# Attention and BitLinear block on eight cores: weight loads ahead of the phase barrier, and another order of the first loads

## The chip, the cores and the metric

One Trainium2 chip, eight cores. Each core computes one of the eight sequences of the batch by itself, with the same program. The metric is the device time of the slowest core, in microseconds (us), as the median of several executions.

## The reference

For each sequence x (4096 tokens, width 1024, f32) the block computes causal attention without separate projections, and a feed-forward part with quantized weights and activations, each followed by a layer norm without gain:

```
encR   = x @ R
A      = softmax(encR @ x.T + causal mask)
x1     = layernorm(x + A @ x)
h      = gelu(bitlinear(x1, W1, b1))          # 1024 -> 4096
out    = layernorm(x1 + bitlinear(h, W2, b2)) # 4096 -> 1024

bitlinear(x, W, b):
    w_scale = max(mean(|W|), 1e-5)
    Wq = clip(round(W / w_scale), -1, 1) * w_scale
    x_scale = max(max over the row |x|, 1e-5)
    xq = clip(round(x * 127 / x_scale), -128, 127) * x_scale / 127
    return xq @ Wq.T + b
```

## The kernel before

The program is written out for five engines (PE, DVE, ACT, POOL, SP) by a small builder. `b.op` puts an instruction on an engine, `b.dma` puts a transfer on the queue of SP ("sync"), ACT ("scalar") or POOL ("gpsimd"). Each names the regions it reads and writes, and the builder makes waits from them: a reader waits for the last writers, a writer for writers and readers, an `accum_writes` only for readers. Each engine runs its list in order, so what is written first also waits first. DMAs take their semaphores in turn from a pool of 7 (SP, POOL) or 5 (ACT), and a DMA waits until the one that used its semaphore before has landed. `b.barrier()` makes every engine wait for all instructions and for all DMAs put down so far; its list of DMA counts is taken at its place in the program (`_pool_targets`).

The sequence is cut into 32 tiles of 128 tokens and 8 groups of 512 (group g holds tokens 512g to 512g+511).

**Start.** For group g, `emit_enc_loads(g)` loads four tiles token-major to bf16 (`etm(k)`, POOL's queue, which converts from f32), `emit_enc_stores(g)` writes them to `enc_bf` in HBM, and `emit_enc_transp(g)` reads them back feature-major with eight DMA transposes (`efm(c)` of group g); stores and transposes are on SP's queue. R is brought to a bf16 layout in HBM, `r_bfT`, in eight steps: POOL loads a row block (to `rstage` or `rstage2`, in turn), ACT's queue stores it. `Rcol(0)` and `Rcol(1)` are two buffers for blocks of `r_bfT`, loaded on SP; the first load waits for all eight stores.

**Attention (lines 629 to 665).** Tiles run in the order 4, 5, ..., 31, 0, 1, 2, 3 (`order`, with SKIP = 4), and the groups in the order 1, 2, ..., 7, 0 (`mstream`). At each fourth tile, `emit_encR` computes x @ R for a group in eight e-steps: Rcol times `efm` (L531), eight matmuls each. The first one is for group 1, so it needs Rcol(0) and the eight transposes of group 1. Scores (L546) need `efm` of all groups up to the tile's own; the exponentials go to `A_sb`, are transposed on PE (L575) and multiplied with `etm` (L592, L598). The residual tile comes into `eres`, `emit_epiA` (L606 to L626) writes y1 = x + A x to `y1pre_h`, on SP, from `y1p`.

**Preparation of the weights.** `drain_prep` puts 130 steps between the tiles: W1 and W2 are read once for the mean of their absolute values (loads to `wslot`, DVE L414), then again to be rounded (L452, L456, L459) and stored as bf16 to `w1q_h` and `w2q_h`, with loads and stores on POOL's queue. The steps of W2's rounding come last, and the last of them stand behind the last tile.

**Turn.** Lines 667 to 680: the barrier; then on POOL the bias rows; on SP the eight loads of W1 (`w1tb(d)`, 1 MB each, over the place of the `etm` tiles 4d to 4d+3); and on SP and ACT in turn the eight loads of W2 (1 MB each, the k-th over the place of `efm(k)`). Then ACT takes logarithm and exponential of the variances (L681, L683), and the feed-forward part begins with the loads of `y1t(0)` and `y1t(1)` (lines 869 to 873). `y1t(0)` has the place of `eres(0)`, `y1t(1)` that of `eres(1)`.

**Feed-forward part.** For each tile: `emit_quant` on DVE (L697 to L736), PE transposes, `emit_mm1_half` (8 matmuls L757 with W1 and one with the bias row, L763, to each group of 512 outputs; then Gelu on ACT, L768, and a maximum on DVE, L772), `emit_roundh`, transposes, `emit_mm2` with W2 (L823, L827), `emit_epiB`. Mm1 of tile i+1 is put ahead of mm2 of tile i. The last stage normalizes and writes the output.

The barrier's list of targets, which both versions share:

```
def _pool_targets(self):
    t = []
    for q, pool in self.pools.items():
        for j, s in enumerate(pool["sems"]):
            uses = (pool["n"] - 1 - j) // len(pool["sems"]) + 1 \
                if pool["n"] > j else 0
            if uses > 0:
                t.append((s, 16 * uses))
    return t
```

Of the kernel before, what the change touches and what calls it, by code (L numbers as in the profile page):

```python
# [160 lines left out]
def build_nc(NT=32, npart=None):  # L161
# [28 lines left out]
    with stack:  # L190
# [16 lines left out]
        b = Builder(nc, stack)  # L207
# [26 lines left out]
        def Rcol(s):  # L234
            return bf_med[:, abase + 2048 + 1024 * s:abase + 2048 + 1024 * (s + 1)]
# [122 lines left out]
        b.dma("gpsimd", mask_sb[:, :], maskc[:, :], writes=["mask"])  # L358
        emit_enc_loads(SKIP // 4 if NT >= 8 else 0)
        b.dma("sync", ident[:, :], identi[:, :], writes=["ident"])  # L360
        b.dma("sync", ones_sb[:, :], ones_i[:, :], writes=["ones"])
        for d in range(8):
# [6 lines left out]
                  reads=[rg], accum_writes=["rbfT"])  # L369
        g1st = SKIP // 4 if NT >= 8 else 0  # L370
        emit_enc_loads(1 - g1st)
        emit_enc_loads(2)
        emit_enc_loads(3)
        emit_enc_stores(g1st)
        emit_enc_transp(g1st)
        b.dma("sync", Rcol(0), r_bfT[0], reads=["rbfT"], writes=["Rcol0"])
        emit_enc_stores(1 - g1st)
        emit_enc_transp(1 - g1st)
        emit_enc_stores(2)
# [87 lines left out]
        k = 0  # L467
# [198 lines left out]

        b.barrier()
        b.dma("gpsimd", b1row2, b1bc[0:2, :], writes=["b1row2"])
        b.dma("gpsimd", b2row2, b2bc[0:2, :], writes=["b2row2"])
        for d in range(8):  # L670
            b.dma("sync", w1tb(d), w1q_h[128 * d:128 * (d + 1), :],
                  reads=["w1qh"], writes=[f"w1q{d}"])
        for k in range(8):
            dst = bf_big[:, 32768 + 4096 * k:32768 + 4096 * (k + 1)].rearrange(
                "p (r c) -> p r c", r=4)
            src = w2q_h[512 * k:512 * (k + 1), :].rearrange(
                "(r p) c -> p r c", r=4, p=128)
            b.dma("sync" if k % 2 == 0 else "scalar", dst, src,
                  reads=["w2qh"],
                  writes=[f"w2q{4 * k + j}" for j in range(4)])  # L680
        b.op("scalar", lambda s: s.activation(lnu[:, 0:NT], uA[:, 0:NT], AF.Ln),  # L681
# [158 lines left out]
        def emit_epiB(i):  # L840
# [27 lines left out]

        b.dma("gpsimd", y1t(0), y1pre_h[0:128, :], reads=["y1h0"],
              writes=["y1t0"])  # L870
        if NT > 1:
            b.dma("gpsimd", y1t(1), y1pre_h[128:256, :], reads=["y1h1"],
                  writes=["y1t1"])
        emit_quant(0)
# [100 lines left out]
```

How the kernel before makes its waits and increments, by code:

```python
            def go(eng):  # L144
                for waits, fn, incspec in self.ops[name]:
                    for sem, val in waits:
                        eng.wait_ge(sem, val)
                    if fn is None:
                        continue
                    inst = fn(eng)
                    if incspec is not None:
                        inst.then_inc(incspec[0], incspec[1])
```

## Time and profile before

| | us |
|---|---|
| time, median of 3 runs | 2499.88 |
| lowest and highest of the 3 | 2493.76, 2558.49 |
| execution that was profiled: time | 2494.65 |
| the same: span of the slowest core (core 0) | 2493.1 |
| the same: spans of the other cores | 2474.4 to 2490.7 |

The profile is of core 0 in one execution; its times count from the core's first instruction. The span and the execution's own time differ by 1.55 us, which lie around the instructions. A span is read in three parts here: the start to about 131 us, the attention part to about 1065, the turn to about 1130, and the feed-forward part and the output behind it.

In the rows, L110 is the builder's line for all plain DMAs and L108 for transposes, so a DMA is known by what it moves: "enc_bf<-bf_big" is a store of a tile, "bf_med<-r_bfT" a load of Rcol, "bf_big<-w1q_h" a load of W1. SPq, ACTq and POOL rows of DMAs are the time to issue them, not to move them. q0 is the queue of POOL, q1 that of SP, q10 that of ACT.

### The profile page before, as it was taken

The numbers are of one execution on the slowest core, as the hardware profiler recorded it, in microseconds if no ns is written. First come the engines' busy times: TensorE is split into PE (matmuls) and PEld (weight loads), VectorE is DVE, ScalarE is ACT, GpSimd is POOL, SyncE is SP. The second block draws the span as 40 slices with busy tenths as digits, with TensorE's granted clock in tenths as the row PEclk, the third lists the DMA queues.
The fourth block names the chain that finished last, engine by engine and source line by source line (L and its number), as shares of the span: only waits on it lengthen the run. The fifth ranks groups of instructions, "written<-read, shape, count | busy, mean of one in ns | idle before, by whom it ended". The sixth has DMA issues, their size and how long they took to land.

```text
span 2493.1 us, 27352 instructions; the slowest of 8 cores (2474.4 to 2493.1 us)
## 1 busy us (share of the span) xinstructions
PE 1847.4 (74%) x8840; PEld 798.3 (32%) x9016; DVE 974.2 (39%) x1941; ACT 641.9 (26%) x1271; POOL 169.2 (7%) x303
## 2 busy tenths in 40 slices
PE   0257778887896985117998989998899998988930
PEld 0123233343342432003333333333333343333310
DVE  0042241324232332425445454554545455454422
ACT  0022232232231321003323232232323323232210
POOL 2011111101111111110000000000000000000000
PEclk9878899998998998558999999999999999999975
DMA  9676746546656453573000000000000000000038
GB/s 153 157 199 199 202 168 170 178 106 142 119 134 159 102 144 97 139 242 125 26 13 26 26 14 26 13 26 26 14 26 13 26 14 26 26 14 26 5 125 288
DMA packets 124027, 232.77 MB, mean 93 GB/s; under 512 B 52076, under 2 KB 52204, under 8 KB 122862
## 3 DMA queue, kind: packets, MB, share of 16 engines
q0 software_dynamic: 42832, 128.20, 20.4%
q1 hardware_dynamic: 66016, 88.14, 11.2%
q10 hardware_dynamic: 15040, 14.68, 2.1%
q8 instruction: 75, 1.23, 0.2%
q14 instruction: 64, 0.52, 0.1%
HBM read 164.11 MB, written 69.21 MB: 94 GB/s over the span
## 4 chain that ended last, share of the span: by engine, by line
PE 60%; DMA 21%; issue 7%; DVE 6%; ACT 4%; SPq 1%; POOL 1%; DVEq 0%; ACTq 0%; another core or an unknown queue 0%; POOLq 0%
PE psc L757 16%; PE pav L827 9%; PE pav L823 9%; PE psc L546 6%; DMA bf_med<-r_bfT 6%; PE ptp L575 5%; PE psc L531 4%; PE pav L592 4%; PE pav L598 3%; PE psc L763 3%; DMA w1q_h<-f_big 3%; DMA w2q_h<-f_big 3%; DMA bf_med<-y2pre_h 3%; ACT bf_med L582 2%; DMA f_big<-w1t 2%
## 5 line engine op out<-in xcount | busy, mean ns | idle before, releaser
L757 PE MATMUL psc<-bf_big,bf_med 128*128 128x512 bf16 x1984 | 484.6, 383 | 10.0 <-DMA bf_big<-w1q_h 5.9
L827 PE MATMUL pav<-bf_big,bf_med 128*128 128x512 bf16 x1023 | 397.0, 388 | 4.6 <-ACT bf_med L582 1.3
L823 PE MATMUL pav<-bf_big,bf_med 128*128 128x512 bf16 x977 | 379.3, 388 | 1.0 <-ACT bf_med L582 0.9
L531 PE MATMUL psc<-bf_big,bf_med 128*128 128x512 bf16 x502 | 156.1, 470 | 212.0 <-DMA bf_med<-r_bfT 207.3
L546 PE MATMUL psc<-bf_big,bf_med 128*128 128x512 bf16 x1126 | 280.4, 390 | 1.5 <-issue 0.2
L575 PE MATMUL ptp<-ident,bf_med 128*128 128x128 bf16 x1808 | 169.9, 222 | 129.5 <-ACT bf_med L582 64.5
L768 ACT ACTIVATE f_big<-psc,stats 128x512 f32<-128x512 f32 x256 | 176.0, 687 | 345.8 <-PE psc L763 338.3
L772 DVE TENSOR_REDUCE stats<-f_big 128x1 f32<-128x512 f32 x256 | 169.5, 683 | 231.7 <-ACT f_big L768 231.7
L757 PEld LDWEIGHTS psc<-bf_big,bf_med 128*128 128x128 bf16 x2048 | 181.5, 98 | 239.0 <-issue 57.0
L559 ACT ACTIVATE bf_med<-psc,stats 128x512 bf16<-128x512 f32 x144 | 99.2, 689 | 384.5 <-DVE psc L554 189.5
L575 PEld LDWEIGHTS ptp<-ident,bf_med 128*128 128x128 bf16 x1808 | 118.1, 98 | 206.4 <-issue 174.9
L554 DVE TENSOR_TENSOR psc<-psc,mask_sb 128x512 f32<-128x512 f32 x32 | 22.3, 696 | 412.9 <-PE psc L546 318.8
L582 ACT COPY bf_med<-ptp 128x512 bf16<-128x512 bf16 x320 | 172.4, 587 | 22.9 <-PE ptp L575 9.7
L592 PE MATMUL pav<-bf_big,bf_med 128*128 128x512 bf16 x221 | 87.3, 395 | 113.1 <-ACT bf_med L585 99.8
L851 ACT ACTIVATE f_big<-bf_med 128x1024 f32<-128x1024 bf16 x32 | 33.8, 1056 | 519.4 <-DVE bf_med L846 519.4
L846 DVE SCALAR_TENSOR_TENSOR bf_med<-pav,stats,f_big 128x1024 bf16<-128x1024 f32 x32 | 41.1, 1284 | 321.5 <-PE ptp L807 271.5
L546 PEld LDWEIGHTS psc<-bf_big,bf_med 128*128 128x128 bf16 x1152 | 114.1, 100 | 135.1 <-issue 14.9
L531 PEld LDWEIGHTS psc<-bf_big,bf_med 128*128 128x128 bf16 x512 | 55.9, 115 | 309.1 <-issue 281.2
L823 PEld LDWEIGHTS pav<-bf_big,bf_med 128*128 128x128 bf16 x1024 | 102.5, 100 | 125.8 <-issue 13.9
L827 PEld LDWEIGHTS pav<-bf_big,bf_med 128*128 128x128 bf16 x1024 | 102.4, 100 | 122.9 <-issue 10.2
L592 PE MATMUL pav<-bf_big,b1b 128*128 128x512 bf16 x293 | 112.1, 382 | 20.7 <-ACT b1b L585 18.4
L763 PE MATMUL psc<-b1b,rows 2*128 2x512 bf16 x256 | 98.6, 385 | 32.3 <-ACT rows L744 32.2
(112 smaller groups left out, 1538.1 us busy)
## 6 DMA issues: line engine op xcount, KB each, us to landing
f_big<-w1t POOLq DMA_DIRECT2D x64, 512.0 KB, 5.7
f_big<-w2t POOLq DMA_DIRECT2D x64, 512.0 KB, 5.0
f_big<-enc POOLq DMA_DIRECT2D x32, 512.0 KB, 6.4
bf_med<-r_bfT SPq DMA_DIRECT2D x64, 256.0 KB, 4.5
y1pre_h<-f_big SPq DMA_DIRECT2D x32, 512.0 KB, 2.9
f_big<-y1pre_h POOLq DMA_DIRECT2D x32, 512.0 KB, 3.8
out<-f_big SPq DMA_DIRECT2D x32, 512.0 KB, 3.9
bf_big<-enc POOLq DMA_DIRECT2D x32, 256.0 KB, 11.5
```

Of the source, the lines that this page charges most:

```text
L531: lambda t, e=e, d=d, cur=cur, qlo=qlo, bk=bk: t.matmul(psc[bk][:, :], Rcol(cur)[:, 128 * d:128 * (d + 1)], efm(d, qlo, qlo + 512), start= ...
L546: lambda t, e=e, sup=sup, bank=bank, qi=qi: t.matmul(psc[bank][:, :], encR(e)[:, 128 * (qi % 4):128 * (qi % 4 + 1)], efm(e, 512 * sup, 512 ...
L559: s.activation(A_sb(p)[:, 512 * sup:512 * (sup + 1)], psc[bank][:, :], AF.Exp, bias=bcn, accum_out=sums4[:, sup:sup + 1]),
L575: b.op("tensor", lambda t, j=j, bb=bb: t.transpose(ptp[pk][:, 128 * j:128 * (j + 1)], src_ap[:, 128 * bb:128 * (bb + 1)], ident[:, :]), re ...
L582: b.op("scalar", lambda s, n=n: s.copy(dst2, ptp[pk][:, 0:n]), reads=[f"ptp{pk}"], accum_writes=[dst_region])
L592: b.op("tensor", lambda t, j=j, bb=bb, g=g, nb=nb: t.matmul(pav[:, 0:512], ATg(g)[:, 128 * j:128 * (j + 1)], etm(bb)[:, 0:512], start=(bb ...
L757: b.op("tensor", lambda t, d=d, s4=s4, sup=sup: t.matmul(psc[s4][:, :], xq_fm[:, 128 * d:128 * (d + 1)], w1tb(d)[:, 512 * sup:512 * (sup + ...
L763: b.op("tensor", lambda t, s4=s4, sup=sup, i=i: t.matmul(psc[s4][:, :], s1row2(i % 2), b1row2[:, 512 * sup:512 * (sup + 1)], start=False, ...
L768: b.op("scalar", lambda s, s4=s4, sup=sup, i=i: s.activation(hbuf(512 * sup, 512 * (sup + 1)), psc[s4][:, :], AF.Gelu, scale=s1c[:, i % 2: ...
L772: b.op("vector", lambda v, sup=sup: v.reduce_max(habs[:, sup:sup + 1], hbuf(512 * sup, 512 * (sup + 1)), axis=AXX, apply_absolute_value=True),
L823: b.op("tensor", lambda t, c=c: t.matmul(pav[:, 0:512], hq_fm[:, 128 * c:128 * (c + 1)], w2tb(c)[:, 0:512], start=(c == 0), stop=False), r ...
L827: b.op("tensor", lambda t, c=c: t.matmul(pav[:, 512:1024], hq_fm[:, 128 * c:128 * (c + 1)], w2tb(c)[:, 512:1024], start=(c == 0), stop=False),
```

## The change

It has two parts. At the turn, the loads of the bias rows, of W1 and of W2 are put down ahead of the barrier, and so are the loads of `y1t(0)` and `y1t(1)`, which stood at the beginning of the feed-forward part. As no barrier stands between them and the attention part, they name the regions whose place they take: the `ATG` and `rstage2` buffers, `eres`, the `etm` tiles and the `efm` blocks. At the start, group 0 is loaded first and once more behind R, then group 1; and group 0 is stored and transposed ahead of the first Rcol load, group 1 behind it. The order of the tiles and of `emit_encR` is the same.

```
--- before.py
+++ after.py
@@ -356,7 +356,7 @@
                       transpose=True)
 
         b.dma("gpsimd", mask_sb[:, :], maskc[:, :], writes=["mask"])
-        emit_enc_loads(SKIP // 4 if NT >= 8 else 0)
+        emit_enc_loads(0)
         b.dma("sync", ident[:, :], identi[:, :], writes=["ident"])
         b.dma("sync", ones_sb[:, :], ones_i[:, :], writes=["ones"])
         for d in range(8):
@@ -367,15 +367,15 @@
                   r_bfT[:, :, 128 * d:128 * (d + 1)].transpose([1, 0, 2]),
                   stg.rearrange("p (e j) -> p e j", e=8),
                   reads=[rg], accum_writes=["rbfT"])
-        g1st = SKIP // 4 if NT >= 8 else 0
-        emit_enc_loads(1 - g1st)
+        emit_enc_loads(0)
+        emit_enc_loads(1)
+        emit_enc_stores(0)
+        emit_enc_transp(0)
+        b.dma("sync", Rcol(0), r_bfT[0], reads=["rbfT"], writes=["Rcol0"])
         emit_enc_loads(2)
+        emit_enc_stores(1)
+        emit_enc_transp(1)
         emit_enc_loads(3)
-        emit_enc_stores(g1st)
-        emit_enc_transp(g1st)
-        b.dma("sync", Rcol(0), r_bfT[0], reads=["rbfT"], writes=["Rcol0"])
-        emit_enc_stores(1 - g1st)
-        emit_enc_transp(1 - g1st)
         emit_enc_stores(2)
         b.dma("gpsimd", eres(0), enc[128 * order[0]:128 * (order[0] + 1), :],
               writes=["eres0"])
@@ -664,12 +664,19 @@
             drain_prep((oi + 1) / (1.0 * NT))
         drain_prep(1.0)
 
-        b.barrier()
-        b.dma("gpsimd", b1row2, b1bc[0:2, :], writes=["b1row2"])
+        b.dma("gpsimd", b1row2, b1bc[0:2, :],
+              writes=["b1row2"] + [f"ATG{s}" for s in range(2, 8)]
+              + ["rstage2"])
         b.dma("gpsimd", b2row2, b2bc[0:2, :], writes=["b2row2"])
+        b.dma("gpsimd", y1t(0), y1pre_h[0:128, :], reads=["y1h0"],
+              writes=["y1t0", "eres0"])
+        if NT > 1:
+            b.dma("gpsimd", y1t(1), y1pre_h[128:256, :], reads=["y1h1"],
+                  writes=["y1t1", "eres1"])
         for d in range(8):
             b.dma("sync", w1tb(d), w1q_h[128 * d:128 * (d + 1), :],
-                  reads=["w1qh"], writes=[f"w1q{d}"])
+                  reads=["w1qh"],
+                  writes=[f"w1q{d}"] + [f"etm{k}" for k in range(4 * d, 4 * d + 4)])
         for k in range(8):
             dst = bf_big[:, 32768 + 4096 * k:32768 + 4096 * (k + 1)].rearrange(
                 "p (r c) -> p r c", r=4)
@@ -677,7 +684,9 @@
                 "(r p) c -> p r c", r=4, p=128)
             b.dma("sync" if k % 2 == 0 else "scalar", dst, src,
                   reads=["w2qh"],
-                  writes=[f"w2q{4 * k + j}" for j in range(4)])
+                  writes=[f"w2q{4 * k + j}" for j in range(4)]
+                  + [f"efm{k}g{g}" for g in range(NG)])
+        b.barrier()
         b.op("scalar", lambda s: s.activation(lnu[:, 0:NT], uA[:, 0:NT], AF.Ln),
              reads=["uA"], writes=["lnu"])
         b.op("scalar", lambda s: s.activation(rstdA[:, 0:NT], lnu[:, 0:NT],
@@ -866,11 +875,6 @@
             b.dma("sync", y2pre_h[128 * i:128 * (i + 1), :], y2st(i % 2),
                   reads=[f"y2st{i % 2}"], writes=[f"y2h{i}"])
 
-        b.dma("gpsimd", y1t(0), y1pre_h[0:128, :], reads=["y1h0"],
-              writes=["y1t0"])
-        if NT > 1:
-            b.dma("gpsimd", y1t(1), y1pre_h[128:256, :], reads=["y1h1"],
-                  writes=["y1t1"])
         emit_quant(0)
         emit_xqT(0)
         emit_s1rows(0)
```

The instructions as they now stand, at the places that matter. First POOL's queue at the start, a piece of the difference; "bf_med<-r_mat" and "b1b<-r_mat" are the last two loads of R, "bf_big<-enc" are loads of encoding tiles, "f_big<-enc" is the first residual tile:

```order
 L110 DMA bf_med<-r_mat 128x1024
 L110 DMA b1b<-r_mat 128x1024
-L110 DMA bf_big<-enc 128x1024 x12
+L110 DMA bf_big<-enc 128x1024 x16
 L110 DMA f_big<-enc 128x1024
 L110 DMA bf_big<-enc 128x1024 x4
```

Four more tiles are loaded behind R, sixteen where there were twelve.

Next SP's queue at the start, a piece of the difference with the semaphores that are waited for. The names in it don't tell the group: the four stores are of group 1 before and of group 0 now.

```order
 L110 DMA ident<-identi 128x128
 L110 DMA ones_sb<-ones_i 128x1
-L110 DMA enc_bf<-bf_big 128x1024 [waits dp_gpsimd1]
-L110 DMA enc_bf<-bf_big 128x1024 [waits dp_gpsimd2]
-L110 DMA enc_bf<-bf_big 128x1024 [waits dp_gpsimd3]
-L110 DMA enc_bf<-bf_big 128x1024 [waits dp_gpsimd4]
+L110 DMA enc_bf<-bf_big 128x1024 [waits dp_gpsimd6]
+L110 DMA enc_bf<-bf_big 128x1024 [waits dp_gpsimd0]
+L110 DMA enc_bf<-bf_big 128x1024 [waits dp_gpsimd1]
+L110 DMA enc_bf<-bf_big 128x1024 [waits dp_gpsimd2]
 L108 DMA_TRANSPOSE bf_big<-enc_bf 128x512 [waits dp_sync2,dp_sync3,dp_sync4,dp_sync5]
 L108 DMA_TRANSPOSE bf_big<-enc_bf 128x512 [waits dp_sync0]
```

The kinds and their order on SP are the same in both; the first stores waited for POOL's transfers 1 to 4 (the mask is 0), the first loads of all, and now wait for its transfers 13 to 16, which are the second loads of group 0 behind R.

Last ACT's list at the turn, before:

```order
L110 DMA bf_big<-w2q_h 128x4x1024 x3
L681 ACTIVATE stats<-stats 128x32
L683 ACTIVATE stats<-stats 128x32 [waits es_scalar]
L582 COPY bf_med<-ptp 128x512 [waits es_tensor] x2
L744 COPY rows<-ptp 2x128 [waits es_tensor]
```

and now:

```order
L110 DMA bf_big<-w2q_h 128x4x1024 [waits dp_scalar4,dp_sync1,dp_sync2,dp_sync0]
L110 DMA bf_big<-w2q_h 128x4x1024 [waits dp_scalar0,dp_sync4,dp_sync3,dp_sync2]
L110 DMA bf_big<-w2q_h 128x4x1024 [waits dp_sync4]
L690 ACTIVATE stats<-stats 128x32 [waits es_scalar,es_vector,es_tensor,dp_sync0,dp_sync1,dp_sync2,dp_sync3,dp_sync4,dp_sync5,dp_sync6,dp_gpsimd3,dp_gpsimd4,dp_gpsimd5,dp_gpsimd6,dp_scalar0,dp_scalar1,dp_scalar2,dp_scalar3,dp_scalar4]
L692 ACTIVATE stats<-stats 128x32 [waits es_scalar]
L582 COPY bf_med<-ptp 128x512 [waits es_tensor] x2
```

The long list of waits is the barrier's. Before, it stood at ACT's first load of W2; now it stands at the logarithm behind the loads, and it holds all semaphores of SP's and ACT's queues, on which the weights arrive. The first DVE instruction behind the barrier has such a list too.

## Rows read from the trace of the kernel before

**Rows 1.** The page: its head, and section 4, the chain's shares by engine.
```profile
span 2493.1 us, 27352 instructions; the slowest of 8 cores (2474.4 to 2493.1 us)
...
PE 60%; DMA 21%; issue 7%; DVE 6%; ACT 4%; SPq 1%; POOL 1%; DVEq 0%; ACTq 0%; another core or an unknown queue 0%; POOLq 0%
```

**Rows 2.** Chain of waits, 40 to 135 us: start, length, what.
```profile
48.90 29.65 DMA r_bfT<-b1b
...
106.85 5.77 PE psc L531 x16
...
131.30 1.23 DVE stats L414
```

**Rows 3.** Timeline, 0 to 135 us: start, length, engine, line, operation, [idle before <-releaser].
```profile
19.36 11.35 SPq L108 DMA_TRANSPOSE bf_big<-enc_bf  x8
...
42.88 3.18 POOL L110 DMA_DIRECT2D bf_big<-enc  x6
...
78.72 0.34 SPq L110 DMA_DIRECT2D bf_med<-r_bfT  x1
...
86.65 3.57 PE L531 MATMUL psc<-bf_big,bf_med 128*128 128x512 bf16 x8 [86.65 <-DMA bf_med<-r_bfT]
88.83 10.25 SPq L108 DMA_TRANSPOSE bf_big<-enc_bf  x8
...
101.71 21.11 SPq L110 DMA_DIRECT2D bf_med<-r_bfT  x8
```

**Rows 4.** DMA queues, 50 to 60 us: packets, MB, share of 16 engines.
```profile
q0 software_dynamic: 820, 1.49, 96.4%
q10 hardware_dynamic: 799, 0.20, 14.7%
```

**Rows 5.** The same, 20 to 30 us.
```profile
q0 software_dynamic: 288, 0.52, 41.1%
q1 hardware_dynamic: 2720, 0.66, 38.4%
```

**Rows 6.** The same, 90 to 100 us.
```profile
q1 hardware_dynamic: 4222, 1.02, 54.3%
```

**Rows 7.** Windows: length, busy (x) of PE, PEld, DVE, ACT, POOL, then PEclk, DMA share, GB/s.
```profile
1088.00:1092.00 4.00, 0.00 (x0) 0.00 (x0) 0.00 (x0) 0.00 (x0) 2.64 (x5) 0.50 0.68 184
...
1130.00:1140.00 10.00, 10.00 (x40) 3.63 (x39) 4.24 (x6) 4.00 (x6) 0.00 (x0) 0.91 1.05 387
1140.00:1144.00 4.00, 3.95 (x18) 1.42 (x17) 2.74 (x14) 1.21 (x2) 0.00 (x0) 1.00 0.53 193
```

**Rows 8.** Chain of waits, 1080 to 1130 us; its columns as in rows 2.
```profile
1083.89 3.62 DMA y1pre_h<-f_big
```

**Rows 9.** Timeline, 1064 to 1158 us; its columns as in rows 3.
```profile
1064.77 0.58 PE L598 MATMUL pav<-bf_big,bf_med 128*128 128x512 bf16 x1
...
1088.03 6.11 SPq L110 DMA_DIRECT2D bf_big<-w1q_h  x8
1088.30 20.44 ACTq L110 DMA_DIRECT2D bf_big<-w2q_h  x4
...
1108.79 0.23 ACT L681 ACTIVATE stats<-stats 128x32 f32<-128x32 f32 x1 [23.67 <-issue]
...
1119.06 2.68 PE L757 MATMUL psc<-bf_big,bf_med 128*128 128x512 bf16 x6 [0.33 <-ACT bf_med L582]
...
1128.54 0.60 PE L763 MATMUL psc<-b1b,rows 2*128 2x512 bf16 x1
...
1132.24 0.38 PE L763 MATMUL psc<-b1b,rows 2*128 2x512 bf16 x1
...
1150.72 3.59 PE L757 MATMUL psc<-bf_big,bf_med 128*128 128x512 bf16 x8
...
1154.25 0.60 PE L763 MATMUL psc<-b1b,rows 2*128 2x512 bf16 x1
...
1157.05 0.38 PE L763 MATMUL psc<-b1b,rows 2*128 2x512 bf16 x1
```

## The prediction

> **What bounds the kernel now.** I read the page first, then the chain of waits, then the timeline at the two places that the change touches, and last the DMA queues there. The page gives PE 60% of the chain that ended last and DMA 21% [rows 1]. These DMA stretches sit at the start and at the turn from attention to the feed-forward part.
>
> At the start the chain runs through the last store of the transposed R, 29.65 us on its way, then through SP's own issues, and PE's second e-step begins at 106.85 [rows 2]. The timeline shows why. The transposes of group 1 were issued at 19.36, long before anyone needed them. Rcol(0) goes out at 78.72 when the R store has landed, PE runs one e-step at 86.65, and then it waits: Rcol(1) is queued on SP behind the stores and eight transposes of group 0 and leaves at 101.71 [rows 3]. Everything later hangs on this. DVE's first weight scan starts at 131.30, behind the first scores [rows 2], and the preparation chain follows it through the whole attention part.
>
> At the turn, PE's last attention matmul begins at 1064.77, but DVE, the weight stores and the last y1 store go on; SP's y1 store is issued at 1083.89 and lands 3.62 later, at 1087.5 [rows 8], and the barrier opens at 1088.03. Then 16 MB of weights come in. ACT is held by issuing its four loads until 1108.79, quantization follows, PE starts at 1119.06 and is paced by w1 until its first group closes at 1128.54 [rows 9]. The weights keep the queues full into the window from 1140 to 1144 [rows 7]; I take 1144 for the last landing: half of them land behind running matmuls. That is the cover which the change takes away.
>
> **The change at the turn.** The weight loads now stand ahead of the barrier, and the barrier collects the latest count of every DMA semaphore. So the first instruction behind it waits for all 16 MB, where before it waited for none of them. Step by step, in the times of this execution:
> - Start of the loads. On SP they are still behind the last y1 store, so they leave at 1083.89 + 0.4 = 1084.3 and not at 1065, where their tiles come free; before, 1088.03. The second half, w2, still waits for the last w2 store. That buys at most 3.7 us. At least it buys what the first 4 us of loading moved before, 184 GB/s x 4 us = 0.74 MB, at the late rate of 387 GB/s: 1.9 us [rows 7]. I take 3: last landing at 1141.
> - Barrier. Before, the y1 store landed at 1087.5 and ACT went on at 1088.30, 0.8 later. Now ACT goes on at 1141.8 with Ln and Exp.
> - Quantization. From 1108.79 to PE's first w1 matmul at 1119.06 was 10.3 us [rows 9]; nothing of it can be done ahead now, since DVE and ACT both stand at the barrier. PE starts at 1152.1.
> - First group. PE has idled since 1065, its granted clock was 0.50 in such a stretch [rows 7] (1.2 GHz of the two levels), and the next group after an idle PE closed 3.5 us after it began (1150.72 to 1154.25 [rows 9]). It closes at 1155.6; before at 1128.54: +27.1.
> - The next group took 3.70 us before (1128.54 to 1132.24) and takes 2.80 after such a start (1154.25 to 1157.05) [rows 9]: -0.9.
>
> Sum: +26, from 24 (3.7 us saved and a little more) to 30. The earlier loads of y1t(0), y1t(1) and the bias rows are worth nothing: they land well before 1141. Taking ACT's 20.44 us of issuing out of the way of Ln is worth nothing either, as ACT now waits for the landings themselves. The POOL, SP and ACT queues hold nothing else that anybody waits for.
>
> **The change at the start.** The order of tiles is unchanged, so PE still needs group 1 first. But now group 0 is loaded first, loaded again behind R, and stored and transposed ahead of Rcol(0) and of group 1. SP's first store waits for the second load, so SP does nothing between 9 and about 47.
> - Gain. The R chain runs without stores and transposes beside it. I take 4 us (bounds 0 and 6): the flood of encoding loads, before from 42.88 [rows 3], begins near 39.
> - Four more loads. One tile is 128 packets, and POOL's queue moved 820 packets in 10 us: 1.56 us a tile, 6.2 us in all [rows 4]. POOL's backlog was 20 loads before (12 tiles, the residual, 4 tiles, 3 weight blocks: 2560 packets, 31 us at this rate, after a slow beginning at 42.88 and with the last ones of twice the size), and I put its end at 84; now 84 - 4 + 6 + 2 (the stores of group 0 beside it) = 88.
> - Transposes of group 0, from about 59, beside that backlog. While it was full, the ACT queue's small packets moved one for one with POOL's, 799 to 820 [rows 4]. One for one, at some 73 per us with three queues, 29 us move about 2100 of the 4096 packets. The other 2000 go at the free rate of 422 per us [rows 6], 5 us: done at 93.
> - Rcol(0) and the stores of group 1 stand behind them in the same queue: about 5 us, 98. From there to Rcol(1) it is as before, 88.83 to 101.71 = 12.9 [rows 3]: 111, so +9.
> - The e = 0 matmuls, before done under this wait, now wait for group 1's transposes and end just before Rcol(1) arrives. They stay hidden; reloading their buffer waits for them, at most 1 us.
>
> Low end: the transposes slip through, Rcol(0) leaves when R has landed, and the R chain is 4 us earlier: -4. High end: they hardly move until 88, end at 98, and with the 18 us behind them give 116, +15, with 2 for the buffer: +17. I take +9, since the row with a full POOL queue is the nearest.
>
> The Trainium skill, *DMA: Bandwidth & Descriptors*, "Queues, rings and completion order", says that a DMA engine goes round its queues by whole packets of about 9 to 17 descriptors, not one by one. The row of R's store shows one small packet for one of POOL's, so the trace does not bear it out there; for transposes I can't exclude it, and by it the start would cost about nothing (first rival).
>
> **Sum.** 26 + 9 = +35. On the execution profiled, 2494.65 us, that is 2530; on the median shown, 2499.88, it is 2535. I take 2533. A measurement of this kernel tells about 2% (50 us) from no change, so this is a loss that stays inside.
>
> **Rivals.**
> 1. *Transposes pass the backlog.* For it: between 20 and 30 us they moved 2720 packets against POOL's 288 [rows 5]. Against it: POOL had only two loads under way then and was idle in part. The start costs 0, the turn 26: 2494.65 + 26 = 2521. Chance 0.24.
> 2. *Slower by over 2%: one queue, one backlog.* SP's queue is in order, so anything that holds group 0's transposes holds R, group 1 and the first scores. If POOL's backlog lasts to 95 (R's store, stores and transposes all taking turns) and the transposes run only after it, 95 + 10 + 18 = 123, +21, and with the turn at its high end of 30: +51. From +50 it decides: 2494.65 + 51 = 2546 on this execution, 2551 on the median. Chance 0.12.
> 3. *Faster: the barrier's new wait is empty.* If it did not cover the loads, or they were issued at 1065 in the shadow of the last weight steps, PE would start on w1's own landing, 3.7 us earlier than before, and with the quicker R chain at the start 4 more: 2494.65 - 8 = 2487. Against it: the barrier takes the counts at its own place in the program, and SP stands at the y1 store until 1083.89 [rows 8]. Chance 0.05.
>
> **Chances.** Forecast (+28 to +45) 0.59, rivals 0.24, 0.12, 0.05. The range for 8 in 10 takes in most of rival 1 and stops where rival 2 begins to be rare: 2514 to 2553. By over 2% slower: 0.12; by over 2% faster: 0.01 (only rival 3 together with something unseen); the rest within 2%.
>
> **What would show it.** Right: no PE instruction from the last attention matmul until some 10 us after the last weight has landed; ACT's Ln at or after 1141 plus the shift of the start; SP's first store past 45; Rcol(1) issued near 111; twenty-four loads in POOL's backlog. Between 131 and 1065 all rows should keep their distances, shifted by the same 9 us; from the first group of the feed-forward part on too. Wrong: DVE's quantization before the weights have landed (rival 3), or Rcol(1) at 98 to 103 (rival 1), or past 120 (rival 2). A shift that shrinks or grows in the middle of the attention part would say that the preparation chain is not tied to the start as I read it.

## The result, and the profile after

The changed kernel takes 2531.37 us (median of 10 runs, 2522.61 to 2592.24); before, run beside it, 2515.86 (10 runs, 2491.59 to 2622.16). The ratio is 1.0145, with a 95% interval of 1.0124 to 1.0166: on the 2499.88 us shown at first that is +36 us, to 2536. In some runs, five of before's ten by their times and one of the changed kernel's, the cores of one half of the chip showed a lower granted clock and a longer time; they pull the medians up, which so differ by 15.5 us only, and every ratio and mean here leaves them out. The forecast was 2533, +33 on the same figure, and within 2%.

The profiled execution took 2522.61 us:

```profile
span 2521.1 us, 27566 instructions; the slowest of 8 cores (2495.1 to 2521.1 us)
...
PE 60%; DMA 20%; issue 7%; DVE 6%; ACT 4%; SPq 2%; POOL 1%; DVEq 0%; ACTq 0%; POOLq 0%
```

The shares stand almost where they stood [rows 1]: 35 us are too few for a share of the span to show. The page of before was of core 0 and this one is of core 7, and the cores of one execution end up to 26 us apart. So I compare places in the program, and take for each the median of the eight cores of the profiled execution.

| median of 8 cores, us | before | after | |
|---|---|---|---|
| first weight scan on DVE (L414) | 128.3 | 140.1 | +11.8 |
| from there to the first W1 load | 944.9 | 937.8 | -7.1 |
| from there to the first group of the feed-forward part closing | 41.2 | 73.0 | +31.8 |
| from there to the end | 1365.6 | 1361.8 | -3.8 |
| end | 2478.4 | 2515.5 | +37.1 |

(The rows are medians of their own and don't add up exactly.) The two places that grew are the two that the change touches.

**The start.** SP's queue on core 7 (start, us on the engine, what, how many):

```profile
45.35 6.17 SPq L110 DMA_DIRECT2D enc_bf<-bf_big  x4
61.14 32.85 SPq L108 DMA_TRANSPOSE bf_big<-enc_bf  x8
94.36 0.33 SPq L110 DMA_DIRECT2D bf_med<-r_bfT  x1
94.85 1.91 SPq L110 DMA_DIRECT2D enc_bf<-bf_big  x4
100.09 10.02 SPq L108 DMA_TRANSPOSE bf_big<-enc_bf  x8
...
112.73 20.90 SPq L110 DMA_DIRECT2D bf_med<-r_bfT  x8
```

SP is idle until the second load of group 0 lands. Then eight transposes hold it for 32.85 us, where the same eight take 10.02 us at 100.09. Rcol(0) leaves at 94.36 where it left at 78.72, and Rcol(1), the first of the eight in the last row, at 112.73 where it left at 101.71 [rows 3]. PE meets that twice, first piece by piece on the transposes of group 1 and then on Rcol(1):

```profile
112.04 0.58 PE L531 MATMUL psc<-bf_big,bf_med 128*128 128x512 bf16 x1 [1.02 <-DMA bf_big<-enc_bf]
116.83 6.40 PE L531 MATMUL psc<-bf_big,bf_med 128*128 128x512 bf16 x16 [4.20 <-DMA bf_med<-r_bfT]
```

The second e-step stood at 106.85 [rows 2] and stands at 116.83. What the transposes shared the DMA engines with is in the queues of 70 to 80 us (first three rows) and 80 to 90 us (packets, MB, share of 16 engines):

```profile
q0 software_dynamic: 751, 1.63, 88.5%
q1 hardware_dynamic: 748, 0.18, 14.7%
q10 hardware_dynamic: 416, 0.10, 5.0%
...
q0 software_dynamic: 709, 1.84, 92.2%
q1 hardware_dynamic: 706, 0.17, 11.2%
```

q1 is SP's queue with the transposes, q0 is POOL's. Their packets go one for one, as the R store's did before [rows 4]; but one of POOL's is some 2 KB and one of SP's 256 bytes or less, so SP gets a tenth of the bytes for half of the packets.

**The turn.** Core 7, from the last y1 store on:

```profile
1084.15 0.32 SPq L110 DMA_DIRECT2D y1pre_h<-f_big  x1
...
1084.98 9.05 SPq L110 DMA_DIRECT2D bf_big<-w1q_h  x8
...
1087.06 21.51 ACTq L110 DMA_DIRECT2D bf_big<-w2q_h  x4
...
1145.87 0.23 ACT L690 ACTIVATE stats<-stats 128x32 f32<-128x32 f32 x1 [60.50 <-issue]
...
1154.12 1.01 PE L575 MATMUL ptp<-ident,bf_med 128*128 128x128 bf16 x8 [89.84 <-DVE bf_med L745]
...
1156.02 3.57 PE L766 MATMUL psc<-bf_big,bf_med 128*128 128x512 bf16 x8 [0.22 <-ACT bf_med L582]
...
1159.52 0.60 PE L772 MATMUL psc<-b1b,rows 2*128 2x512 bf16 x1
...
1161.92 0.39 PE L772 MATMUL psc<-b1b,rows 2*128 2x512 bf16 x1
```

The loads leave 0.8 us after the y1 store where it was 4.1 [rows 8, 9]. Then ACT's logarithm, which came 20.76 us after the first W1 load (1088.03 to 1108.79 [rows 9]), comes 60.9 us after it, and everything of the quantization stands behind it. PE's 89.84 us of idling are put down to DVE L745, the last link; the wait that counts is ACT's, 60.50 us. It is called "issue", since the profile names no single releaser for the barrier's long list. What ended it is read from the windows (the last two columns are the share of the DMA engines and GB/s, ahead of them PE's granted clock, here 0.50, the 1.2 GHz level, in a stretch in which PE did nothing):

```profile
1130.00:1140.00 10.00, 0.00 (x0) 0.00 (x0) 0.00 (x0) 0.00 (x0) 0.00 (x0) 0.50 1.00 321
...
1144.00:1145.00 1.00, 0.00 (x0) 0.00 (x0) 0.00 (x0) 0.00 (x0) 0.00 (x0) 0.50 0.03 12
1145.00:1146.00 1.00, 0.00 (x0) 0.00 (x0) 0.00 (x0) 0.13 (x1) 0.00 (x0) 0.50 0.00 0
```

The engines are full until past 1140, and the last packets of the 16 MB end at 1144.3, while ACT, DVE and PE stand. ACT goes on at 1145.87, 1.5 us behind them. So the barrier opens on the last landing.

### The profile page after: what moved, and what is told of

The parts are those of the page before. It is cut to its first block, busy times and chain, and to the rows that moved or that the text cites. A ratio compares the mean times of both kernels' runs of the same rounds, so it can differ in the third digit from the quotient of the medians.

```text
span 2521.1 us, 27566 instructions; the slowest of 8 cores (2495.1 to 2521.1 us)
## 1 busy us (share of the span) xinstructions
PE 1856.8 (74%) x9016; PEld 797.5 (32%) x9016; DVE 973.9 (39%) x1941; ACT 641.8 (25%) x1271; POOL 171.5 (7%) x307
## 4 chain that ended last, share of the span: by engine, by line
PE 60%; DMA 20%; issue 7%; DVE 6%; ACT 4%; SPq 2%; POOL 1%; DVEq 0%; ACTq 0%; POOLq 0%
PE psc L766 16%; PE pav L832 9%; PE pav L836 9%; PE psc L546 6%; DMA bf_med<-r_bfT 5%; PE ptp L575 5%; PE psc L531 4%; DMA w1q_h<-f_big 4%; PE pav L592 3%; PE psc L772 3%; PE pav L598 3%; DMA w2q_h<-f_big 3%; DMA bf_med<-y2pre_h 2%; ACT bf_med L582 2%; SPq L108 2%
## 5 line engine op out<-in xcount | busy, mean ns | idle before, releaser
L832 PE MATMUL pav<-bf_big,bf_med 128*128 128x512 bf16 x1024 | 398.3, 389 | 1.9 <-ACT bf_med L582 1.9
L836 PE MATMUL pav<-bf_big,bf_med 128*128 128x512 bf16 x1024 | 397.1, 388 | 0.0
L592 PE MATMUL pav<-bf_big,bf_med 128*128 128x512 bf16 x228 | 89.7, 394 | 119.7 <-ACT bf_med L585 106.3
```

The source lines that it names most:

```text
L592: b.op("tensor", lambda t, j=j, bb=bb, g=g, nb=nb: t.matmul(pav[:, 0:512], ATg(g)[:, 128 * j:128 * (j + 1)], etm(bb)[:, 0:512], start=(bb ...
L832: b.op("tensor", lambda t, c=c: t.matmul(pav[:, 0:512], hq_fm[:, 128 * c:128 * (c + 1)], w2tb(c)[:, 0:512], start=(c == 0), stop=False), r ...
L836: b.op("tensor", lambda t, c=c: t.matmul(pav[:, 512:1024], hq_fm[:, 128 * c:128 * (c + 1)], w2tb(c)[:, 512:1024], start=(c == 0), stop=False),
```

## The experiments

Two figures are given for each. The ratio is that of the slowest core to the kernel before on the same chip, with its 95% interval. Since which core is slowest changes from run to run, the mean over the eight cores and over the runs is steadier, and its difference to before is given too, with standard errors near 1.5 us (2.5 for e7_gate). On that measure before is 2478.5 to 2479.4 and the changed kernel 2518.7, about +39. "Group at" is the time from the first W1 load to the first group of the feed-forward part closing, 41.2 before and 73.0 after, and the scan is the first at L414, 128.3 and 140.1; both are medians of the eight cores. The edits are against the kernel before.

**e1_turn: the change's turn alone.** The start is that of before.

```
+        b.dma("gpsimd", b1row2, b1bc[0:2, :],
...
+        for d in range(8):
+            b.dma("sync", w1tb(d), w1q_h[128 * d:128 * (d + 1), :],
...
+        b.barrier()
```

> The start of before, the turn of after. Theory: the two parts of the change add up, and this one carries most of it. From the first W1 load to the close of the first feed-forward group (median of the cores: 41 us before, 73 after) about 72; the loads leave some 3.5 us earlier, so +28 us in all, less 2 to 4 that the feed-forward part gains because no weights arrive beside it: +25. First weight scan at about 128 as before. Rival (the start carries the loss, the turn's waits are mostly the shadow of a transfer that had to end anyway): +10 or less.

Ratio 1.0095 (1.0063 to 1.0126); mean +26.5. Scan 128.5, group at 72.9. The first W1 loads and ACT's logarithm on core 5:

```profile
1083.84 8.30 SPq L110 DMA_DIRECT2D bf_big<-w1q_h  x8
...
1140.70 0.23 ACT L690 ACTIVATE stats<-stats 128x32 f32<-128x32 f32 x1 [56.46 <-issue]
```

The turn is worth what was worked out, 26.

**e2_start: the change's start alone.** The turn is that of before.

```
-        emit_enc_loads(SKIP // 4 if NT >= 8 else 0)
+        emit_enc_loads(0)
...
+        emit_enc_loads(0)
+        emit_enc_loads(1)
+        emit_enc_stores(0)
+        emit_enc_transp(0)
+        b.dma("sync", Rcol(0), r_bfT[0], reads=["rbfT"], writes=["Rcol0"])
```

> The start of after, the turn of before. Theory: the second R block is asked for near 112 instead of 101 us, the first weight scan begins near 140 instead of 128, and the delay is carried to the end: +10 us (between +8 and +13). Rival (the preparation chain in the attention part has slack and swallows it, as the stretch from the first scan to the first W1 load is 7 us shorter after the change than before, of which the earlier issue of the loads explains 3 or 4): +4 or less.

Ratio 1.0014 (0.9988 to 1.0040), which alone tells nothing from none; mean +8.8, from four runs. In the profiled execution the scan is at 141.8, +13.5, and from there to the first W1 load it is 945.0, as before (944.9), so in that execution the delay is carried whole. SP's queue on core 0 is that of the changed kernel:

```profile
44.06 5.68 SPq L110 DMA_DIRECT2D enc_bf<-bf_big  x4
59.39 33.61 SPq L108 DMA_TRANSPOSE bf_big<-enc_bf  x8
```

The two parts make 26.5 + 8.8 = 35 of the 39 of the whole; the rest is about twice the standard error of such a sum, and the 39 sets the whole against other runs of before; by the ratio, taken beside its own runs of before, the whole is 36.

**e3_snap: the turn's loads early, the barrier's list taken before them.** The queue order is that of e1_turn, only what is waited for differs.

```
-    def barrier(self):
+    def targets(self):
...
+    def barrier(self, targets):
...
+        tg = b.targets()
+        b.dma("gpsimd", b1row2, b1bc[0:2, :],
...
+        b.barrier(tg)
```

> The start of before; at the turn the loads ahead of the barrier as in after, but the barrier waits only for what was put down before the loads (the list is taken ahead of them and waited for behind them). Theory: the loss of the turn is the barrier's cover of the 16 MB and nothing else, so it goes, and the earlier issue stays: the first group closes about 37 to 41 us after the first W1 load as before, and that load leaves 3.5 us earlier: -3 us in all. Rival (issuing the loads ahead of everything is itself harmful, by ACT's 20 us of issuing or by loads that crowd out the y1 tiles): as e1_turn, +25, or at least above +8.

Ratio 0.9970 (0.9951 to 0.9989); mean -6.5. Core 5:

```profile
1069.82 9.17 SPq L110 DMA_DIRECT2D bf_big<-w1q_h  x8
...
1071.88 23.40 ACTq L110 DMA_DIRECT2D bf_big<-w2q_h  x4
1096.04 0.23 ACT L692 ACTIVATE stats<-stats 128x32 f32<-128x32 f32 x1 [25.83 <-DMA bf_big<-w1q_h]
...
1111.51 0.38 PE L768 MATMUL psc<-bf_big,bf_med 128*128 128x512 bf16 x1 [1.76 <-DMA bf_big<-w1q_h]
```

ACT goes on after 26 us, when its own issuing (23.40 us for four W2 loads) is over, and PE again waits for W1's last block alone. Group at 41.4. So all of the 26 us lie in the list of the barrier: with the same loads at the same places and another list, 26.5 of loss become 6.5 of gain, 33 us between the two.

**e4_once: the change's start without the second load of group 0.**

```
+        emit_enc_loads(1)
+        emit_enc_stores(0)
+        emit_enc_transp(0)
+        b.dma("sync", Rcol(0), r_bfT[0], reads=["rbfT"], writes=["Rcol0"])
```

> The start of after with group 0 loaded once only, at the very beginning; the turn of before. Theory: what costs at the start is the second load, since SP's stores of group 0 wait for it and everything on SP's queue then runs against POOL's full queue. Without it stores and transposes of group 0 run at 9 to 31 us, the second R block is asked for at 100 to 103 us and the time is that of before, +0 (within 3 us). Rival (the order costs: group 1, which the first products need, is late whatever the loads): +8 or more.

Ratio 1.0005 (0.9985 to 1.0024); mean +0.5; scan 128.6. Core 6:

```profile
20.30 12.61 SPq L108 DMA_TRANSPOSE bf_big<-enc_bf  x8
80.50 0.34 SPq L110 DMA_DIRECT2D bf_med<-r_bfT  x1
...
100.67 19.57 SPq L110 DMA_DIRECT2D bf_med<-r_bfT  x8
```

The order of the groups costs nothing that shows here. The repeated load does, by what waits for it: the stores can't leave at 9 any more, and the transposes fall into POOL's backlog.

**e5_w1only: the list taken between the W1 and the W2 loads.** The barrier covers half of the weights.

```
+                  writes=[f"w1q{d}"] + [f"etm{k}" for k in range(4 * d, 4 * d + 4)])
+        tg = b.targets()
...
+        b.barrier(tg)
```

> As e3_snap, but the list of the barrier is taken behind W1's eight loads and ahead of W2's, so every engine waits for W1 and the bias rows and y1 tiles, not for W2. Theory: W1 lands some 36 us after its first load, then come 0.8 for the barrier, 10.3 for Ln to the first matmul and 3.5 for the first group at the low clock: first group about 51 us after the first W1 load where e3_snap has 41 and e1_turn 73; mean over the cores +3 to +6 us against before. It says how much of the turn's loss is W2's landing (about 22 of 32 us) and how much is quantization that no longer hides behind W1 (10). Rival (the landing of W2 does not matter, the quantization and the cold PE do): first group past 60 us.

Ratio 1.0054 (1.0030 to 1.0078); mean +10.3; group at 54.8. Too little was expected of it. W1's landing (ACT goes on at 1119.52 on core 0, 39.4 us after the first load at 1080.15) is also the start of the 10 us of quantization that ran under it before. The three lists make a scale: none -6.5, W1 +10.3, all +26.5: 16.8 us for the first half of the bytes, 16.2 for the second.

**e6_early: e3_snap, and W1 loaded under the last tiles.** Seven of the eight blocks go out behind the last four epilogues, and W2 wholly on SP.

```
+            for d in {28: (1, 2), 29: (3, 4), 30: (5, 6), 31: (7,)}.get(oi, ()):
+                load_w1(d)
...
-            b.dma("sync" if k % 2 == 0 else "scalar", dst, src,
+            b.dma("sync", dst, src,
```

> As e3_snap, but W1's blocks 1 to 7, whose places come free when tile 31 is done, are loaded one or two at a time between the last small tiles, block 0 behind the last tile, and all of W2 goes on SP's queue, so that ACT issues nothing. Theory: PE waits for W1 only because the loads stand behind the last y1 store; now Ln runs right after the barrier, the first group closes about 14 us after it (before: 41), -26 us, less what 7 MB beside the last weight steps costs that chain (5 to 15 us): -10 to -20 us on the mean over the cores. Rival (the last weight steps are bound by the DMA queues, so all that is gained is given back): -5 or less.

Ratio 0.9994 (0.9967 to 1.0021); mean -5.7, a miss. By the medians of the eight cores, from the last epilogue (L606) to the first group it is 25.8 us where before has 46.6, so the turn is 21 us shorter. But the last stretch of attention, from the epilogue at oi = 28 to the last one, is 122.0 us where it is 107.1. POOL's queue there, core 5 (a POOL load of a W2 block each, and the residual tile):

```profile
1025.38 0.53 POOL L110 DMA_DIRECT2D f_big<-w2t  x1 [6.06 <-DMA w2q_h<-f_big]
1025.90 0.53 POOL L110 DMA_DIRECT2D f_big<-enc  x1
...
1039.57 0.53 POOL L110 DMA_DIRECT2D f_big<-w2t  x1 [12.60 <-DMA w2q_h<-f_big]
...
1046.44 1.02 POOL L110 DMA_DIRECT2D f_big<-w2t  x1 [5.80 <-DMA w2q_h<-f_big]
```

A step of the weight preparation takes 7 us; the one beside which two blocks of W1 were on their way takes 14.2, and the one beside a single block 11.8, from 1061.08 (in before the same kind of step, with the residual tile but without W1, takes 9.0 and 9.4). The preparation chain is the critical one there, and each of its steps waits for its own transfers. The 21 us are bought for 15, and 6 are left.

**e7_gate: both groups ahead of R, group 2 held until R's stores have landed.** The turn is that of before.

```
+        emit_enc_loads(1)
+        emit_enc_loads(0)
...
+        emit_enc_loads(2, ["rbfT"])
...
+        emit_enc_stores(1)
+        emit_enc_transp(1)
+        emit_enc_stores(0)
+        emit_enc_transp(0)
```

> The turn of before. At the start groups 1 and 0 are loaded ahead of R, both stored and transposed while R goes through, and group 2's load waits for all of R's stores, so that POOL's full queue no longer takes turns with them. Theory (small packets go one for one with POOL's, which stretched R's last store to 30 us): R's last store lands in 3 to 6 us at about 52, the first R block arrives at about 57, first weight scan near 95 instead of 128, and as the whole attention part follows it: -25 to -33 us. Rival (the attention part is tied to the DMA traffic of the weights and not to its start): first scan early, but less than 10 us gained.

Ratio 0.9988 (0.9948 to 1.0028); mean -6.1; scan 122.4, where 95 was expected. Core 3:

```profile
24.22 10.38 SPq L108 DMA_TRANSPOSE bf_big<-enc_bf  x8
...
44.73 12.46 SPq L108 DMA_TRANSPOSE bf_big<-enc_bf  x8
67.12 0.33 SPq L110 DMA_DIRECT2D bf_med<-r_bfT  x1
...
79.23 35.59 SPq L110 DMA_DIRECT2D bf_med<-r_bfT  x8
```

Both sets of transposes are now quick, which was the aim. Two things eat it up: R still goes through two staging buffers and is done at 67, and the flood that waits for it meets the eight Rcol loads, which take 35.59 us instead of 19.57. The end follows the scan (-5.9 and -6.1), so the start is critical, as read; only its next waits were not seen.

**e8_both: the edits of e6_early and e7_gate together.**

> e6_early and e7_gate together. Theory: the two parts of the kernel are in a chain and the gains add: -35 to -55 us, a ratio of 0.978 to 0.986. Rival: one gain hides the other, not better than the better of the two by more than 3 us.

Ratio 0.9945 (0.9917 to 0.9973); mean -13.2; -5.7 and -6.1 make -11.8. Within their errors the two add up, so start and turn are independent. The -35 to -55 expected were built on what the two had been expected to give alone.

**e9_w2last: e3_snap, with all of W2 on SP behind W1.**

```
-            b.dma("sync" if k % 2 == 0 else "scalar", dst, src,
+            b.dma("sync", dst, src,
```

> As e3_snap, but all eight W2 loads are on SP's queue behind W1's, instead of half of them on ACT's queue beside W1. Theory: since queues take turns packet by packet, W2 on ACT's queue took its share of the time in which PE waited for W1; alone, W1's 8 MB come in some 22 to 25 us, and the first group closes 27 to 32 us after the first W1 load instead of 41; W2 is not read before some 47 us after the first group and is there by then. Mean over the cores against before -16 to -20 us (e3_snap: -6.5). Rival (the turn is bound by quantization and ACT, W1 is not the last to come): -6 to -8.

Ratio 0.9966 (0.9943 to 0.9989); mean -9.5, a miss; group at 35.0, not 27 to 32. Core 1, windows as above:

```profile
1080.00:1090.00 10.00, 0.00 (x0) 0.00 (x0) 2.11 (x4) 0.00 (x0) 0.00 (x0) 0.50 1.01 301
1090.00:1100.00 10.00, 3.18 (x13) 1.32 (x13) 4.14 (x16) 1.33 (x3) 0.00 (x0) 0.50 0.99 322
1100.00:1110.00 10.00, 1.76 (x3) 0.31 (x3) 0.00 (x0) 0.00 (x0) 0.00 (x0) 0.50 0.99 335
```

ACT is free here; PE's few matmuls of 1100 to 1110 wait for W1's blocks. The queues from 1075 to 1111 tell why W1's 8 MB took 35 us:

```profile
DMA packets 2065, 11.05 MB, mean 307 GB/s; under 512 B 268, under 2 KB 268, under 8 KB 1038
...
q1 hardware_dynamic: 1436, 9.20, 78.1%
q0 software_dynamic: 628, 1.83, 19.7%
```

11 MB moved in that time, 1.83 of them in POOL's queue (the y1t tiles and the last W2 store). What is left of the turn is this transfer; the 27 to 32 us had counted W1's bytes alone, and in 22 to 25 us, which is 336 to 381 GB/s where the mean is 307.

**e10_wide: e7_gate with eight staging buffers for R.** They lie in the place of A_sb, which is not yet in use; R is loaded first of all.

```
+        def rst(d):
+            return A_sb(d // 4)[:, 1024 * (d % 4):1024 * (d % 4 + 1)]
...
+            b.dma("gpsimd", rst(d), r_mat[128 * d:128 * (d + 1), :],
+                  writes=[f"rst{d}"])
```

> The turn of before. At the start R's eight blocks get a buffer each (in the place of the A tiles, which are not in use yet) and are loaded first, so that no load waits for a store; groups 1 and 0 follow, and group 2's load waits for R's stores. Theory: in e7_gate the R chain itself took until 67, by load and store in turn through two buffers; without it the first R block is asked for near 40 and the first weight scan comes near 100 instead of 128; what the scan gains the end gains: -20 to -30 us on the mean over the cores. Rival (the DMA queues are full through the first 90 us whatever the order, so the scan gains 8 us or less, as in e7_gate): -3 to -10.

Ratio 0.9943 (0.9919 to 0.9967); mean -10.8; scan 117.7, a miss, where one near 100 was expected. SP's queue on core 0, and then PE's:

```profile
51.27 0.34 SPq L110 DMA_DIRECT2D bf_med<-r_bfT  x1
51.72 32.05 SPq L108 DMA_TRANSPOSE bf_big<-enc_bf  x8
```

```profile
54.45 3.57 PE L532 MATMUL psc<-bf_big,bf_med 128*128 128x512 bf16 x8 [54.45 <-DMA bf_med<-r_bfT]
90.95 4.29 PE L532 MATMUL psc<-bf_big,bf_med 128*128 128x512 bf16 x12 [32.92 <-DMA bf_med<-r_bfT]
```

R is ready 16 us earlier than in e7_gate, and group 0's transposes stand in the flood again: 32.05 us.

**e11_best: the edits of e9_w2last and e10_wide together.**

> e9_w2last and e10_wide together. Theory: start and turn are in one chain, so the gains add within 3 us. Rival: the gain of the start is lost in the attention part when the turn is changed too (e8_both showed 13 of 12 expected, against it).

Ratio 0.9916 (0.9883 to 0.9949); mean -21.3; the two make -20.3.

**e12_late: e11_best with the flood held back until the last transpose of group 0.** Against e11_best, group 2's stores also move behind the first e-steps.

```
+        emit_enc_transp(0)
+        emit_enc_loads(2, ["efm7g0"])
+        emit_enc_loads(3)
...
+                if mi == 0:
+                    emit_enc_stores(2)
```

> As e11_best, but group 2's load waits for the last transpose of group 0 instead of R's stores, and group 2's stores stand behind the first e-steps on SP's queue. Theory: in e10_wide group 0's eight transposes took 32 us of issuing beside POOL's full queue, as they did after the change (32.85), where alone they take 10; with the flood held back they end near 63, the second R block is asked for at once, and the first weight scan comes at 92 to 100 where e11_best has 118. As the end follows the scan: -14 to -20 us more than e11_best, -35 to -41 on the mean over the cores against before, ratio 0.983 to 0.986. Rival (the work of the queues is only pushed back: weight blocks land later and R blocks run in the flood, so the scan comes at 110 or later): -21 to -26.

2461.61 us (2459.21 to 2463.57, 4 runs) against 2496.66: ratio 0.9878 (0.9847 to 0.9910); mean -28.5; scan 109.4. Core 7:

```profile
52.54 0.33 SPq L110 DMA_DIRECT2D bf_med<-r_bfT  x1
52.97 10.02 SPq L108 DMA_TRANSPOSE bf_big<-enc_bf  x8
63.08 34.48 SPq L110 DMA_DIRECT2D bf_med<-r_bfT  x8
```

In e11_best, on core 0, the second of these rows is this:

```profile
51.69 33.61 SPq L108 DMA_TRANSPOSE bf_big<-enc_bf  x8
```

The same eight transposes at the same place take 10.02 us instead of 33.61. The Rcol loads are in the flood now, 34.48 us, which is why the scan missed the 92 to 100 expected. It beats both kernels: by 1.2% the kernel before, and by 0.9878 / 1.0145 = 0.974, 2.6%, the changed one (worked out from two ratios, not measured side by side).

## Why the prediction was right, and where it was off

**The steps that failed.** The mechanism held at both places. What failed is the last step, behind the sum: that a measurement of this kernel tells about 2% (50 us) from no change, so that the loss stays inside. The interval of the measured ratio, 1.0124 to 1.0166, is 0.4% wide, some 10 us, and a loss of 36 us lies far outside that: it is clearly told from no change. Two terms ahead of it were too small: the start's +9, where Rcol(1) came 11.5 us later by the median of the eight cores, and the 0.8 us between the last landing and ACT, which is 1.5.

**The bound.** Right: both places are critical. A change of the scan comes out at the end whole where the turn is left alone (e7_gate -5.9 and -6.1, e10_wide -10.6 and -10.8; in e2_start's profiled execution 13.5 and 13.9 on the medians), and the stretch from the scan to the first W1 load stays as it was within 4 us (941.3, 947.2 and 945.0; before 944.9). In the changed kernel that stretch is 7 us shorter, of which 3.3 are the earlier issue of the loads. The other 4 are less than single executions differ by: with the start of before, and the loads as early, it is 940.0 in e1_turn, 947.4 in e3_snap and 937.7 in e9_w2last.

**The turn, +26.** Right in size and cause: e1_turn +26.5, and e3_snap takes it all back by the list alone. By its steps: the earlier issue was 3.3 us (3 taken, bounds 1.9 and 3.7). The last landing was taken for 1141 + the shift of the start; on core 0, whose last y1 store is only 2.8 us later (1086.73 and 1083.89), that is 1143.8, and the last packets of the weights end at 1144.2. ACT goes on at 1145.68, 1.5 us behind them where 0.8 was taken. The 0.8 ran from the y1 store's completion, and that came 0.5 us behind its last packet (1087.0), while the 1141 stood for a last packet. From there to PE's first W1 matmul it is 10.15 us (1145.68 to 1155.83; 10.3 taken), and the first group takes 3.5 (1155.83 to 1159.34; 3.5 taken). The second group takes 2.4, not 2.8. From the y1 store to the first group, 72.61 where before had 44.65 [rows 8, 9]: +28.0, 27.1 forecast.

**The start, +9.** Right in its mechanism: the queue ratio (751 to 748, 709 to 706) is the one for one that was assumed of the transposes from the R store's row. By its steps on core 7: the flood began at 37.89, 5 us earlier (4 taken); the transposes went out from 61.14 (59) and were over at 94 (93); Rcol(0) left at 94.36; the transposes of group 1 went out from 100.09 (98), Rcol(1) at 112.73 (111). From Rcol(0) to Rcol(1) it was 18.4 us, 17.9 worked out. By the medians of the eight cores Rcol(1) goes out at 112.1, and in before at 100.6: 11.5 later. The forecast set its 111 against core 0's 101.71, which is 1.1 later than the median; that and the 1.1 us by which 111 was too early are the miss. Nothing was lost behind that: from Rcol(1) to the scan it is 28.0 us, before 27.8, although the e = 0 matmuls run in single pieces until 112.6 on core 7. The scan came 11.8 to 13.5 us late, not 9, and the end 8.8 by the mean of e2_start. The profiled execution of e2_start is the slowest of its four, +12.5 by the mean of its cores where the other three are at +7.6, so its scan need not be theirs. What makes it slower is open.

**The rivals.** *Transposes pass the backlog* fell: 32.85 us against 10.02 in the changed kernel itself, and 33.61 in e11_best against 10.02 in e12_late, where nothing around that place differs but the flood and four stores behind it. The Trainium skill, *DMA: Bandwidth & Descriptors*, "Queues, rings and completion order", has the engine go round its queues by packets of some 9 to 17 descriptors. The equal counts of these rows neither bear that out nor speak against it: turns of as many descriptors on each queue would give them too, and the trace does not say which engine moved what. So the prediction read too much out of that rule when it held the R store's row against it, and again when it said that by it the start would cost about nothing. *Slower by over 2%* did not come: Rcol(1) was at 112.73, not past 120; the transposes were over at 94 and did not first begin there. *The barrier's new wait is empty* fell: 60.50 us of wait. Its counterpart with a true escape, e3_snap, gained 6.5 where 3 were expected; the first group closes as long after its loads as before (41.4 and 41.2), so 3.3 are the earlier issue. The other 3 are about twice the standard error, and its profiled execution does not show them (the median core ends at 2479.1, in before at 2478.4); whether there is more than noise in them is open.

**The sum.** 35 forecast on one execution; +36 by the ratio of the slowest cores, +39 by the mean of all cores, and 35 from the two parts alone.

## What to carry to other kernels

A barrier that collects "the latest count of every queue" turns each prefetch that is issued ahead of it into a wait: take its list before the prefetches, or put them behind it, and ask which landing its first instruction needs. Ask of a flood of loads on one queue which small-packet transfers of others are due beside it, since their packets went one for one with the large ones here: hold the flood back by a dependence (here 23 us in one queue), and then look for the next transfer that it meets. Loading a thing twice costs more than its bytes, for it also moves the earliest moment of all that reads it.

## What the runs showed of the hardware that was not expected

- The eight transposes of group 0 or 1 were issued in 10.0 to 12.8 us with little in POOL's queue, and in 31.9 to 35.3 us beside a full one (all cores of four kernels: after, e2_start, e10_wide, e11_best). The eight Rcol loads: 18.5 to 22.7 us, and 32.4 to 36.8 in the flood (e7_gate, e12_late). The time shows up on SP's queue as issuing and not as waiting.
- Issuing is not cheap for large loads: four W2 loads of 1 MB held ACT's sequencer 19.86 to 23.40 us, about half of the time from their issue to their landing (41.4 us at the median in before), and with that everything that ACT had to compute.
- The 16 MB of weights took 56 to 65 us from the first load's issue to the last packet, whether on two queues (before, after, e3_snap) or on one (e9_w2last, 57.7 to 60.4), with the core's DMA engines at a share near 1. Within that the rate went with what the neighbour did: in the changed kernel's profiled execution core 1 moved 416 GB/s from 1080 to 1090, ahead of core 0's first load at 1087.56, and 299 from 1100 to 1110, beside it; core 0 moved 387 from 1130 to 1140, when core 1 was done (52). Cores 4 and 5 show the same less sharply (core 4: 376 and 304 in these first two windows; core 5: 380 from 1120 to 1130, core 4 142). That the two of a pair take it from each other was not tested by a run.
- A background load of 2 MB under a chain of steps of 7 to 9 us, each of which waits for its own transfers of 256 to 512 KB, lengthened the step beside it to 14.2 us, about 5 more than without it, and one of 1 MB to 11.8, though the stretch as a whole moved only 170 GB/s (e6_early, core 5, 1020 to 1090). What is free on the average isn't free at the moment when the step needs it: from 1025 to 1039 it was 281 GB/s at a share of 0.86.
